# Attention with its weighing of v done for two key tiles in a row in odd steps

## The chip, the core and the metric

One core of a Trainium2 chip runs the whole layer: TensorE (PE) multiplies, ScalarE (ACT), VectorE (DVE) and GpSimd (POOL) work elementwise, SyncE's queue (SP) issues transfers. The metric is the device time of one execution in microseconds. The kernel before took 1863.95 us (median of three runs).

## The reference

A transformer layer with modulation, for 4 sequences of 1024 tokens and width 512, in fp32:

```
shift_msa, scale_msa, gate_msa, shift_mlp, scale_mlp, gate_mlp = split(silu(c) @ Wada.T + bada, 6)
h = modulate(rmsnorm(x, g1), scale_msa, shift_msa)
q, k, v = heads(h @ Wqkv.T + bqkv)              # 16 heads of 32
q = rmsnorm(q, gq) * 32 ** -0.5;  k = rmsnorm(k, gk)
o = softmax(q @ k.T) @ v
x = x + gate_msa * (o @ Wproj.T + bproj)
h = modulate(rmsnorm(x, g2), scale_mlp, shift_mlp)
x = x + gate_mlp * (gelu(h @ Wfc1.T + bfc1) @ Wfc2.T + bfc2)
```

## The kernel before

The kernel has three stages: a short setup, the attention (`build_attention`), and the second half with the output projection and the two large products (`build_mlp`). The change is in the attention alone.

The attention is one long row of 256 steps, L = 0 to 255, with 18 more (negative L) ahead of them for the first projections. A step is one key tile of 128 keys against 512 queries, for four heads at once. Eight steps (eight key tiles) make one half: four heads and 512 queries; 16 steps make one group of four heads, 64 steps one sequence. Each engine walks the same steps in its own order, which is written out by hand, and waits on semaphores for the others.

PE does in step L, in this order: `qk(L, 0)`, the scores of two heads (two matmuls); the first half of `fill`; `qk(L, 1)`, the scores of the other two heads; the row sums, in one step of eight; the second half of `fill`; in some steps a sum of squares or a turn; and at the end `weigh(L - 1)`, which multiplies the exponentials of the step before with v. A weighing is four 128x32 matmuls, one a head, into the four quarters of one PSUM bank; the profile shows each as two instructions. The row sums (`row_sums`) are 128x32 groups too, of ones with the summed exponentials. All else on PE has 128x128 weights.

`fill` does the projections that the coming groups and the next sequence need. `PLAN` lists them: units (q or k of four heads for 512 tokens) and tiles of v, each of 12 matmuls spread over two steps (six a step) or three (four a step). They all go through one PSUM bank, `gemm`. The first matmul of the next unit waits (`gemm_free`) until DVE has taken the last one out (`raw_out`, `v_out`). Every step from 1 to 207 has such projection work; steps 208 to 255 have none. A unit of q or k then goes on through square (ACT), sum of squares (PE), logarithm and root (ACT), the parts (DVE), and over DRAM into `k_stack` and `q_stack`. A turn (`turn`) transposes a normalised tile of x on PE.

ACT does the two exponentials of step L (`exponentials`), each for two heads, as soon as their scores are there. They go to a ring of three buffers `probs`, so that the exponential of step L waits for the weighing of step L - 3. PE's scores of a step wait for the exponential of the step before that reads the same PSUM tensor.

DVE adds up the exponentials (`add(L - 1)` in its step L, not for a half's first tile), and takes the projections out, in the order of its own list. The row sums of a half (`ROWS_AT`, the second step of the next half, always an odd one) need its last addition, and DVE's first addition of the next half needs the row sums.

Names in the profile: L456 scores, L469 weighing (`pv`), L486 row sums, L493 sum of squares, L500 turn, L521 and L534 projections, L616 exponentials, L681 additions, L712 and L722 the projection taken out, L767 and L769 parts.

Of the kernel before, what the change touches and what calls it, by code (L numbers as in the profile page):

```python
# [93 lines left out]
FILL = {step + i: (kind, b, g, x, i, steps) for step, steps, b, kind, g, x in PLAN for i in range(steps)}  # L94
# [8 lines left out]
def at_row(when):  # L103
    return {NT * (hh + 1) + when: hh for hh in range(NC * NG - 1)}


ROWS_AT, COMPACT_AT, INVERT_AT, INVERTED_AT, SPREAD_AT, OUT_AT = (at_row(x) for x in (ROWS, COMPACT, INVERT, INVERTED, SPREAD, OUT))
OUT_AT[AFTER + 1] = NC * NG - 1

TURN = list(range(-17, -9)) + [15, 19, 21, 23, 27, 35, 39, 45]  # L110
for b in range(2, B):
    TURN += [BSTEPS * b - 78 + 8 * t for t in range(NT)]
TURN_AT = {step: n for n, step in enumerate(TURN)}
STAT_AT, HOUT_AT, SPLIT_AT = ({step + after: n for step, n in TURN_AT.items()} for after in (-1, 1, 2))
MOD_AT = {TURN[NT * b - 1] + 2: b for b in range(1, B)}

# [156 lines left out]
def build_attention(nc, small, dram, wq_hi, wq_lo):  # L273
# [4 lines left out]
    with ExitStack() as ctx:  # L278
# [160 lines left out]
        def _(pe):  # L439
            issued = dict(units=0, v=0, squares=0, turns=0, rows=0)  # L440

            def qk(L, p):
                group, st = L // STEPS, L % STEPS
                half, j = st // NT, st % NT
                s = group % 2
                if p == 0:
                    if st == 0 or st == NT // 2:
                        pe.wait_ge(k_in[s][st // (NT // 2)], 64 * (group // 2 + 1))
                    if j == 0:
                        pe.wait_ge(q_in[half], 64 * (group + 1))  # L450
                if L > 0:

                    pe.wait_ge(exp_done, 2 * (L - 1) + p + 1)
                for i in range(2):
                    h = 2 * p + i
                    mm = nc.tensor.matmul(scores[p][:, i, :], k_stack[s][:, h, j * P:(j + 1) * P], q_stack[half][:, h, :],  # L456
                                          start=True, stop=True)
                mm.then_inc(qk_mm, 1)

            def weigh(l):  # L460
                b, g, j, hh = l // BSTEPS, l // STEPS % NG, l % NT, l // NT
                pe.wait_ge(exp_done, 2 * l + 2)
                if l % BSTEPS < NT:
                    pe.wait_ge(v_moved, b * NT + j + 1)
                if j == 0 and hh >= NH:

                    pe.wait_ge(o_done, hh - NH + 1)
                for h in range(HG):
                    mm = nc.tensor.matmul(pv[hh % NH][h * DH:(h + 1) * DH, :], v[b % 2][:, j, (g * HG + h) * DH:(g * HG + h + 1) * DH],  # L469
                                          probs[l % RING][:, h, :], start=(j == 0), stop=(j == NT - 1))  # L470
                mm.then_inc(pv_mm, 1)

            def aux_free():

                if issued["squares"]:
                    pe.wait_ge(ln_done, issued["squares"])
                if issued["turns"]:
                    pe.wait_ge(h_moved, issued["turns"])
                if issued["rows"]:
                    pe.wait_ge(rows_moved, issued["rows"])  # L480

            def row_sums(hh):
                pe.wait_ge(added, ADDS * (hh + 1))
                aux_free()
                for h in range(HG):
                    mm = nc.tensor.matmul(aux[h * DH:(h + 1) * DH, :], small["ones"][:], sums[:, h, :], start=True, stop=True)  # L486
                mm.then_inc(rs_mm, 1)
                issued["rows"] += 1

            def sum_squares(n):  # L490
                pe.wait_ge(sq_done, n + 1)
                aux_free()
                nc.tensor.matmul(aux[:], small["head_ones"][:], squares[:], start=True, stop=True).then_inc(ss_mm, 1)  # L493
                issued["squares"] += 1

            def turn(n):
                pe.wait_ge(x_normed, n + 1)
                aux_free()
                for k in range(KT):
                    mm = nc.tensor.transpose(aux[:, k * P:(k + 1) * P], xt[n % XS][:, k * P:(k + 1) * P], small["ident"][:])  # L500
                mm.then_inc(turned, 1)
                issued["turns"] += 1
# [36 lines left out]
            def fill(L, part):  # L539
                if L not in FILL:  # L540
                    return
                kind, b, g, x, i, steps = FILL[L]
                per = 3 * KT // steps
                lo = i * per + part * (per // 2)
                hi = lo + per // 2
                if kind == "v":
                    v_products(b, x, lo, hi)
                else:
                    unit_products(kind, b, g, x, lo, hi)

            for L in range(START, AFTER):
                if L >= 0:
                    qk(L, 0)
                fill(L, 0)
                if L >= 0:
                    qk(L, 1)
                if L in ROWS_AT:
                    row_sums(ROWS_AT[L])
                fill(L, 1)
                if L in SUM_AT:  # L560
                    sum_squares(SUM_AT[L])
                if L in TURN_AT:
                    turn(TURN_AT[L])
                if L > 0:
                    weigh(L - 1)
                if L == ADA_MM:
                    for k in range(KT):
                        for i, r in enumerate(ada_rows):
                            if k == 0:
                                pe.wait_ge(ada_w_in[i], 16)  # L570
                            mm = nc.tensor.matmul(scores[0][r, 0, :], silu[:, k, :], ada_w[i][:, k, :], start=(k == 0), stop=(k == KT - 1))
                    mm.then_inc(ada_mm, 1)
                if L == -1:

                    pe.wait_ge(ada_made, NA_LATER)
# [808 lines left out]
```

## Time and profile before

| | |
|---|---|
| median of three runs | 1863.95 us (1860.57 to 1865.57) |
| the profiled execution | 1864.95 us, span 1863.2 us |
| PE busy | 1760.5 us, 94% |
| DVE busy | 1101.3 us, 59% |
| ACT busy | 921.3 us, 49% |
| POOL busy | 363.3 us, 19% |
| attention, steps 1 to 255 | about 95 to 1005 us |
| of these, steps with projections | 95 to 877 us |

Times in the rows are microseconds from the span's start. PE's busy time is that of overlapping matmuls, with modelled ends: the distance between two starts tells what a matmul costs, not its duration. PEld is the loading of weights, which runs beside the matmuls. DVE and ACT are unevenly used: most of their work is in the attention. "Idle before" in brackets is the engine's idle time in front of a row and what ended it; "issue" is time in which the engine waited for nothing that the profile shows.

### The profile page before, as it was taken

What the parts mean: (1) busy time and instruction counts of PE and PEld (TensorE: products, weight loads), DVE (VectorE), ACT (ScalarE), POOL (GpSimd) and SP (SyncE); (2) the same over time, 40 slices, a digit from 0 to 9 for tenths busy, and PEclk for the clock granted to TensorE, in tenths of its full rate; (3) what the DMA queues carried; (4) which work ended last, traced back from release to release, by engine and by line L of the source; (5) the groups of instructions that cost most, each with busy time, mean ns of one, the idle gap of its engine ahead of it and who ended that gap; (6) DMA issues with size and microseconds to landing.
All of it is one profiled execution on the core that took longest, in us unless ns stands there. A gap on an engine that the chain in (4) does not pass through costs nothing. (4 is left out here: it accounts for less than half of the span.)

```text
span 1863.2 us, 23267 instructions
## 1 busy us (share of the span) xinstructions
PE 1760.5 (94%) x8368; PEld 1139.4 (61%) x8368; DVE 1101.3 (59%) x1343; ACT 921.3 (49%) x1110; POOL 363.3 (19%) x296
## 2 busy tenths in 40 slices
PE   3899899999999999999995799999999999999998
PEld 1555454555555555544231577888888787878786
DVE  4578878888898888878785654223232414232311
ACT  2277577777777777777885432222121222122221
POOL 1100100010110110000000432324241424233331
PEclk7999999999999999999997799999999999999999
DMA  5555535556555555454563331202020201001000
GB/s 184 153 146 142 138 107 139 137 138 157 132 132 144 135 144 128 126 133 137 132 134 103 116 102 40 63 6 62 17 62 17 62 17 51 28 30 44 6 29 23
DMA packets 137611, 176.69 MB, mean 95 GB/s; under 512 B 33668, under 2 KB 58244, under 8 KB 137528
## 3 DMA queue, kind: packets, MB, share of 16 engines
q1 hardware_dynamic: 122472, 158.79, 32.1%
q10 hardware_dynamic: 15056, 16.81, 2.8%
q8 instruction: 50, 0.82, 0.2%
q14 instruction: 33, 0.27, 0.1%
HBM read 124.63 MB, written 50.92 MB: 94 GB/s over the span
## 5 line engine op out<-in xcount | busy, mean ns | idle before, releaser
L616 ACT ACTIVATE probs<-scores,shift 128x1024 f32<-128x1024 f32 x512 | 549.7, 1115 | 195.6 <-PE scores L456 191.8
L681 DVE TENSOR_TENSOR sums<-sums,probs 128x2048 f32<-128x2048 f32 x192 | 444.5, 2315 | 45.0 <-ACT probs L616 40.7
L456 PE MATMUL scores<-q_stack,k_stack 128*128 128x512 f32 x1024 | 345.7, 423 | 6.6 <-ACT probs L616 6.5
L456 PEld LDWEIGHTS scores<-q_stack,k_stack 128*128 128x128 f32 x1024 | 169.6, 188 | 254.4 <-ACT probs L616 133.3
L1148 PE MATMUL acc<-w_hi,act_parts 128*128 128x512 f32 x1024 | 317.4, 391 | 0.0
L469 PE MATMUL pv<-probs,v 128*32 128x512 f32 x2048 | 274.3, 608 | 0.4 <-ACT probs L616 0.4
L1111 POOL TENSOR_TENSOR act_parts<-act_full,act_parts 128x512 fp32r<-128x512 f32 x128 | 169.6, 1325 | 501.7 <-ACT act_parts L1062 501.0
L1055 ACT ACTIVATE act_full<-up,f_bias 128x512 f32<-128x512 f32 x128 | 88.3, 690 | 337.7 <-PE up L1165 317.0
L1148 PEld LDWEIGHTS acc<-w_hi,act_parts 128*128 128x128 f32 x1024 | 190.7, 188 | 38.6
L1165 PE MATMUL up<-z_hi,w_hi 128*128 128x512 f32 x512 | 201.5, 394 | 5.1 <-POOL z_lo L1098 5.1
L1165 PE MATMUL up<-z_lo,w_hi 128*128 128x512 f32 x512 | 200.3, 391 | 0.0
L1165 PE MATMUL up<-z_hi,w_lo 128*128 128x512 f32 x512 | 200.2, 391 | 0.0
L1148 PE MATMUL acc<-w_lo,act_parts 128*128 128x512 f32 x512 | 199.4, 389 | 0.0
L1223 DVE TENSOR_TENSOR y_next<-proj,p_bias 128x512 f32<-128x512 f32 x28 | 19.3, 690 | 297.2 <-PE proj L1126 297.2
L1062 ACT ACTIVATE act_parts<-act_full 128x512 fp32r<-128x512 f32 x128 | 81.2, 635 | 222.1 <-PE acc L1148 221.0
L521 PE MATMUL gemm<-h_hi,wqkv_hi 128*128 128x512 f32 x256 | 103.9, 406 | 14.4 <-issue 11.6
L1165 PEld LDWEIGHTS up<-z_hi,w_hi 128*128 128x128 f32 x512 | 96.9, 189 | 25.5 <-POOL z_lo L1098 5.5
L469 PEld LDWEIGHTS pv<-probs,v 128*32 128x32 f32 x2048 | 41.1, 108 | 114.7 <-ACT probs L616 62.2
L658 POOL TENSOR_TENSOR x_inv<-x_sqc,minus_half 128x1 f32<-128x1 f32 x32 | 17.6, 551 | 475.9 <-DVE x_sqc L733 475.9
L1165 PEld LDWEIGHTS up<-z_lo,w_hi 128*128 128x128 f32 x512 | 97.0, 189 | 20.1
L1165 PEld LDWEIGHTS up<-z_hi,w_lo 128*128 128x128 f32 x512 | 96.8, 189 | 20.4
L1148 PEld LDWEIGHTS acc<-w_lo,act_parts 128*128 128x128 f32 x512 | 96.1, 188 | 20.2
(134 smaller groups left out, 2092.9 us busy)
## 6 DMA issues: line engine op xcount, KB each, us to landing
parts_scratch<-parts SPq DMA_DIRECT2D x64, 512.0 KB, 3.1
k_stack<-parts_scratch SPq DMA_DIRECT2D x128, 256.0 KB, 4.9
q_stack<-parts_scratch SPq DMA_DIRECT2D x128, 256.0 KB, 5.1
xt<-in_x SPq DMA_DIRECT2D x32, 256.0 KB, 2.9
heads_out<-o_out SPq DMA_DIRECT2D x32, 256.0 KB, 4.7
out<-result SPq DMA_DIRECT2D x32, 256.0 KB, 2.0
inverse<-inverse_scratch SPq DMA_DIRECT2D x124, 64.0 KB, 2.0
heads<-heads_out SPq DMA_DIRECT2D x30, 256.0 KB, 3.3
```

Of the source, the lines that this page charges most:

```text
L456: mm = nc.tensor.matmul(scores[p][:, i, :], k_stack[s][:, h, j * P:(j + 1) * P], q_stack[half][:, h, :], start=True, stop=True)
L469: mm = nc.tensor.matmul(pv[hh % NH][h * DH:(h + 1) * DH, :], v[b % 2][:, j, (g * HG + h) * DH:(g * HG + h + 1) * DH], probs[l % RING][:, h ...
L521: mm = nc.tensor.matmul(gemm[:], w[:, k, at:at + P], h[:, k, c], start=(n == 0), stop=(n == len(terms) - 1))
L616: nc.scalar.activation(probs[L % RING][:, 2 * p:2 * p + 2, :], scores[p][:], ACT.Exp, bias=small["shift"][:]).then_inc(exp_done, 1)
L658: nc.gpsimd.tensor_tensor(x_inv[:, t:t + 1], x_sqc[:, t:t + 1], small["minus_half"][:, 0:1], ALU.pow).then_inc(inv_done, 1)
L681: nc.vector.tensor_tensor(sums[:], a[:], probs[l % RING][:], ALU.add).then_inc(added, 1)
L1055: nc.scalar.activation(act_full[m % 2][:], up[m % 2][:], ACT.Gelu_apprx_tanh, bias=f1_bias[:, m:m + 1]).then_inc(gelu_done, 1)
L1062: nc.scalar.activation(act_parts[m % 2][:, 0, :], act_full[m % 2][:], ACT.Copy).then_inc(act_hi, 1)
L1111: nc.gpsimd.tensor_tensor(act_parts[m % 2][:, 1, :], act_full[m % 2][:], full(act_parts[m % 2][:, 0, :]), ALU.subtract).then_inc(act_lo, 1)
L1148: mm = nc.tensor.matmul(acc[t][:], act_parts[m % 2][:, b, t * P:(t + 1) * P], w2[a][:, m, :], start=(m == 0 and i == 0), stop=(m == NM - 1 ...
L1165: mm = nc.tensor.matmul(up[m % 2][:], w1[a][:, k, m * P:(m + 1) * P], z[b][:, k, :], start=(k == 0 and i == 0), stop=(k == KT - 1 and i == 2))
L1223: nc.vector.tensor_tensor(yt, proj[:], p_bias[:], ALU.add).then_inc(proj_moved, 1)
```

## The change

In steps up to 207 (`PAIRED`, the last one with projections) PE no longer weighs one tile at the end of each step. It weighs none in an even step and two in an odd one: `weigh(L - 2)` and `weigh(L - 1)`. The row sums of a half move from the middle of their step to directly in front of these weighings. From step 208 on the order is as before. No other engine's code is changed, and nothing is added or removed.

```
+PAIRED = max(FILL)
+assert PAIRED % 2 == 1
...
                 fill(L, 0)
                 if L >= 0:
                     qk(L, 1)
-                if L in ROWS_AT:
+                if L in ROWS_AT and L > PAIRED:
                     row_sums(ROWS_AT[L])
                 fill(L, 1)
                 if L in SUM_AT:
                     sum_squares(SUM_AT[L])
                 if L in TURN_AT:
                     turn(TURN_AT[L])
-                if L > 0:
+                if L in ROWS_AT and L <= PAIRED:
+                    row_sums(ROWS_AT[L])
+                if L > PAIRED:
+                    weigh(L - 1)
+                elif L > 0 and L % 2 == 1:
+
+                    if L > 1:
+                        weigh(L - 2)
                     weigh(L - 1)
```

## Rows read from the trace of the kernel before

**Rows 1.** Busy us by stretch: length, each engine (instructions), clock, DMA, GB/s

```profile
93.17:150.31 57.14, 56.33 (x278) 30.29 (x276) 43.60 (x40) 43.53 (x48) 0.00 (x0) 1.00 0.54 139
150.31:332.62 182.31, 169.31 (x836) 89.08 (x833) 153.21 (x187) 124.70 (x142) 16.82 (x18) 0.98 0.50 133
332.62:877.09 544.47, 543.00 (x2807) 278.98 (x2803) 464.13 (x464) 409.82 (x453) 45.23 (x30) 1.00 0.53 136
```

**Rows 2.** PE's timeline, steps with projections: start, us, what, idle before

```profile
501.65 0.39 PE L534 MATMUL gemm<-wqkv_hi,h_lo 128*128 128x512 f32 x1
501.97 1.07 PE L469 MATMUL pv<-probs,v 128*32 128x512 f32 x8
502.97 0.73 PE L456 MATMUL scores<-q_stack,k_stack 128*128 128x512 f32 x2
503.54 0.39 PE L534 MATMUL gemm<-wqkv_hi,h_hi 128*128 128x512 f32 x1
...
504.23 0.62 PE L456 MATMUL scores<-q_stack,k_stack 128*128 128x512 f32 x2
504.69 0.39 PE L534 MATMUL gemm<-wqkv_hi,h_hi 128*128 128x512 f32 x1
...
505.38 1.02 PE L493 MATMUL aux<-squares,head_ones 128*128 128x512 f32 x2
506.32 1.07 PE L469 MATMUL pv<-probs,v 128*32 128x512 f32 x8
```

**Rows 3.** Timeline of all engines in the tail, where row sums stand before a weighing

```profile
944.93 1.06 PE L486 MATMUL aux<-sums,ones 128*32 128x512 f32 x8
945.39 0.13 PEld L469 LDWEIGHTS pv<-probs,v 128*32 128x32 f32 x4 [0.30 <-ACT probs L616]
945.82 1.04 PE L469 MATMUL pv<-probs,v 128*32 128x512 f32 x8
...
946.79 0.96 PE L456 MATMUL scores<-q_stack,k_stack 128*128 128x512 f32 x3
```

**Rows 4.** PE's timeline, steps 88 to 91

```profile
450.16 0.72 PE L456 MATMUL scores<-q_stack,k_stack 128*128 128x512 f32 x2
...
454.80 1.07 PE L486 MATMUL aux<-sums,ones 128*32 128x512 f32 x8
455.79 0.50 PE L521 MATMUL gemm<-h_hi,wqkv_hi 128*128 128x512 f32 x1
456.13 0.39 PE L521 MATMUL gemm<-h_lo,wqkv_hi 128*128 128x512 f32 x1
...
459.18 0.39 PE L521 MATMUL gemm<-h_hi,wqkv_lo 128*128 128x512 f32 x1
...
461.50 0.40 PE L521 MATMUL gemm<-h_hi,wqkv_hi 128*128 128x512 f32 x1
```

**Rows 5.** DVE's timeline, steps 88 to 91

```profile
453.77 0.69 DVE L761 SCALAR_TENSOR_TENSOR raw<-norms,raw 128x512 f32<-128x512 f32 x1 [0.84 <-ACT norms L591]
...
457.24 0.55 DVE L738 TENSOR_SCALAR xt<-xt,x_inv,x_gain 128x512 f32<-128x512 f32 x1 [0.66 <-POOL x_inv L658]
...
459.90 0.74 DVE L712 TENSOR_SCALAR raw<-gemm,qk_bias 128x512 f32<-128x512 f32 x1
```

**Rows 6.** ACT's timeline, step 88

```profile
451.01 2.12 ACT L616 ACTIVATE probs<-scores,shift 128x1024 f32<-128x1024 f32 x2 [1.04 <-PE scores L456]
```

**Rows 7.** Timeline of all engines where a unit ends in step 140

```profile
638.55 0.75 DVE L712 TENSOR_SCALAR raw<-gemm,qk_bias 128x512 f32<-128x512 f32 x1 [0.78 <-PE gemm L521]
...
640.01 0.39 PE L521 MATMUL gemm<-h_hi,wqkv_hi 128*128 128x512 f32 x1
```

**Rows 8.** PE's timeline, step 23

```profile
190.37 0.48 PE L521 MATMUL gemm<-h_hi,wqkv_hi 128*128 128x512 f32 x1 [2.00 <-issue]
...
191.08 0.63 PE L521 MATMUL gemm<-h_hi,wqkv_lo 128*128 128x512 f32 x1
```

**Rows 9.** ACT's timeline, step 149

```profile
670.07 0.69 ACT L587 ACTIVATE norms<-aux,ln_floor 128x512 f32<-128x512 f32 x1 [2.41 <-DVE raw L761]
```

## The prediction

> **What bounds the kernel.** The page's first part says that PE is busy for nearly all of the span, but that is pipelined matmuls overlapping each other and doesn't say what one of them costs. So I began with the busy time by stretch [rows 1]. The change acts in the 207 steps with projections: steps 1 to 15 (57.1 us), 16 to 55 (182.3 us), 56 to 207 (544.5 us). In the last, PE is at its full clock and never idle for long, DVE is at 464.1 of 544.5 us (85%) and ACT at 75%. In the middle one PE is busy for 169.3 of 182.3 us, and DVE holds it up in nine steps. So PE's own work sets the time in most of the stretch, with DVE some 15% behind it.
>
> Next, PE's timeline inside steps [rows 2]. Two score matmuls and the next projection product are 0.46 us apart when nothing was switched (504.23 to 504.69), 0.23 us each. Around the weighing it is slower: the last product starts at 501.65, the weighing at 501.97, 0.09 us later than a pitch of 0.23; from there to the scores takes 1.00 us; the scores then take 0.57 us to the next product, 0.11 more than the undisturbed pair. The 128x32 groups of a weighing thus cost 1.20 us in a step.
>
> **What two in a row save.** Two such groups stand directly behind each other in the tail, where there is no projection between the row sums and the weighing: 944.93 to 945.82 is 0.89 us, and 945.82 to the scores at 946.79 is 0.97 us [rows 3]. Together 1.86 us, against 2 x 1.00 apart; and one entry (0.09) and one exit (0.11) go as well: 0.34 us a pair. The kinds of row differ (the first is the row sums, whose weights are all ones), but shapes and type are the same, so I take this price. At the low end of what it could be, only entry and exit go (0.20).
> Odd steps 3 to 207 are 103 pairs: 103 x 0.34 = 35.0 us. Step 1 weighs one tile alone.
>
> The Trainium skill (TensorE: Matmul & The Clock Gate, The mechanism) says that weight loads overlap running matmuls only where they go to other row groups; here every tile uses all 128 rows. The trace disagrees: the loads of the weighing start at 945.39, in the middle of the row sums [rows 3]. By the page the second group would start only when the first is over, at 1.06 us instead of 0.89, and the 103 pairs would bring 17.5 us in place of 35.0.
>
> **Row sums.** They now stand in the middle of a filled step: 0.99 us from 454.80 to the next product at 455.79, 0.34 from it to the one after, 0.11 over the pitch [rows 4], and with the entry of 0.09 that is 1.19 us. Directly in front of the weighing they cost 0.89 [rows 3]. 25 of them stand at or before step 207: 25 x 0.30 = 7.5 us. They come up to 1 us later in their step, but the new place is still in front of two weighings; ACT's copy of them and DVE's first addition of the next group wait for them, and both have until the next scores. Cost taken: nothing; without that cover a few tenths in each of 25 steps.
>
> No instruction is added or removed, no DMA is touched, and SP's and POOL's queues stay as they are. PE's gross gain is 42.5 us. Now what the weighing covered.
>
> **Exponentials.** An even step has no weighing. With four products it lasts 0.57 + 0.92 + 0.46 = 1.95 us. ACT's two exponentials of that step start 0.85 us after its first scores and end at 2.97 (451.01 + 2.12 against 450.16) [rows 4, 6]. The next step's second scores need the last: due at 1.95 + 0.92 = 2.87, free at 3.01. That is 0.14 us in each even step of four products with no turn or sum of squares at its end, 22 that end no projection unit: 3.1 us, of which two lie in the middle stretch. With six products the step is 2.41 us and nothing waits. The ring of three probability buffers costs nothing: the exponential of an even step needs the first weighing of the step before, which PE has done before it starts the scores.
>
> **The hand-over of the projection's bank.** This is the larger one. There is one bank for the projection, so the first product of a unit waits until DVE has taken the unit before. A unit that ends in an odd step gets more cover than now (two weighings), one that ends in an even step loses 1.2 us. Of 84 units 51 end in an even step. Kinds:
> - 12 with nothing behind their last product. DVE takes the bank at 638.55 for 0.75 us, and the next product at 640.01 comes 0.71 us after that [rows 7]. Of the 1.20 us of cover 0.5 was needed: 12 x 0.5 = 6.0 us.
> - 12 with a turn behind. For seven of them (steps 90, 98, 106, 114, 154, 162, 170) DVE's order decides. In the first, counted from 450.16: DVE's chain starts with the parts at 453.77, which wait for ACT's second exponential and root of that same even step, so PE's change doesn't bring it forward. It runs on, with one POOL wait of 0.66, to 459.90, and the bank is free at 460.64, +10.48 [rows 5]. PE will come earlier: step 88 takes 1.95, step 89 1.84 + 0.14 + 0.09 + 0.89 + 0.89 + 0.97 = 4.82, step 90 1.95 + 0.44 for the turn (461.50 less 459.18 is 2.32; less 0.23, 0.09, 0.99 and 0.57 it is 0.44 [rows 4]). With the scores it is at +9.62 and waits to +10.53: 0.9 us. 7 x 0.9 = 6.3 us, the others 0.4.
> - 27 with a sum of squares behind (505.38 to 506.32, less the entry: 0.85 us [rows 2]), which leaves 1.15 us to DVE's 0.8. Free where DVE comes at once; it doesn't in the middle stretch.
>
> **The middle stretch.** In nine of its steps PE now waits for DVE's copy, as at 190.37, 2.00 us [rows 8]. DVE's finish doesn't move when PE is quicker. And the weighing that stood ahead of that wait stands behind it now, so 0.9 us of cover becomes 0.9 us of work after it. What DVE still gains is that it sometimes waits for PE in turn. Of 20 x 0.34 + 5 x 0.30 = 8.3 us I keep 4.
>
> Two more pairs bring nothing: behind steps 84 and 148 ACT's logarithm waits for DVE (2.41 us before 670.07 [rows 9]), with the exponentials behind it in ACT's order and PE's next scores behind those: 0.7 us.
>
> **Sum.** Steps 1 to 15: 7 x 0.34 + 0.30 = 2.7, less 0.5 (step 2) and 0.6 (step 14): 1.6. Middle: 4. Steps 56 to 207: 76 x 0.34 + 19 x 0.30 = 31.5, less 20 x 0.14 = 2.8, 8 x 0.5 = 4.0, 6.3 + 0.4, 1.2 for two ends with a late DVE, 0.7: 16.1. Together 21.7 us. The profiled execution took 1864.95 us (span 1863.2), 1.0 above the median 1863.95; 1864.95 - 21.7 = 1843.25, and 1842 on the median's scale. I take 1843.
>
> **Rivals.**
> - *The whole 42.5 us* (chance 0.1): DVE's copies hide after all, since DVE's additions start earlier by the moved weighing. For it: DVE is idle for 15%. Against: the bank at 638.55 [rows 7], where DVE comes at once and still needs 0.75. About 1823 (1818 to 1829).
> - *DVE takes it all* (0.12): its waits for POOL and ACT (0.66 and 0.84 us [rows 5]) can't shrink. If it stays at 85 to 87%, steps 56 to 207 need 464.1 / 0.87 = 533 to 545 us, at most 11 us less than now; with 0 to 2 from the rest, 1852 to 1863. Against: nothing in PE's or DVE's order fixes that share.
> - *Second group as slow as the page's rule has it* (0.06; the trace speaks against it): a pair is 1.06 + 0.97 = 2.03 and with entry and exit saves 0.17, so 42.5 becomes 25.0; with the same losses, 20.8 us, the time would be about 1861.
> - *Slower* (0.05): the hand-over without cover. If each of the 51 even ends costs the whole 1.20 us, that is 61 us against 42.5: 1883. It decides from 0.84 us an end; the kinds above need 0.5 for the commonest and 0.9 for seven. In the middle stretch it could come true, since PE's idle time there grows from 2.0 to nearly 3 us, and after such a wait a product takes 0.63 us instead of 0.40, and the granted clock of the stretch is 0.98 [rows 1, 8].
> - *The forecast* (0.67): its own range 1834 to 1851, from the middle stretch at 0 to 8 us, the hand-over at half or all again.
>
> **Numbers.** Change by over 0.3% is 5.6 us, about what a measurement of this kernel can tell. Range 1829 to 1857. Faster 0.87, same 0.08, slower 0.05.
>
> **What would show it.** After: from a pair's first weighing to the second about 0.89 us, from there to the scores 0.97 to 1.00; even steps of four products near 1.95 to 2.0 us; a wait of 0.5 us before the first product after units ending in even steps, released by DVE; 0.9 us at the seven turn steps; DVE at 87 to 89% in steps 56 to 207; the tail and the second stage as long as now. I am wrong if the weighing pair is 2.0 us or more, if PE's waits for DVE or ACT in steps 56 to 207 sum to over 25 us or under 8, or if more of the middle stretch runs at the lower clock.

## The result, and the profile after

The changed kernel takes 1848.78 us (median of six executions, 1847.01 to 1852.23), the kernel before 1863.29 (six, 1860.57 to 1865.57). The ratio is 0.9927, 95% interval [0.9916, 0.9938]: 13.6 us less by the ratio, between 11.6 and 15.7 (the two medians are 14.5 apart). The profiled execution took 1848.84 us with a span of 1847.0. Forecast were 1843 us and a range of 1829 to 1857.

The page's first part, engine by engine (busy us, share of the span, instructions):

```profile
PE 1729.6 (94%) x8368; PEld 1154.5 (63%) x8368; DVE 1101.5 (60%) x1343; ACT 913.2 (49%) x1110; POOL 358.7 (19%) x296
```

PE is busy for 31 us less than before, while the span is only 16 us shorter. PE's busy time fell by twice as much as came out at the end; the rest went into waits. The windows of the same stretches as [rows 1] say where:

```profile
147.64:327.08 179.44, 162.53 (x843) 92.69 (x841) 153.89 (x188) 124.90 (x145) 19.42 (x18) 0.99 0.52 136
327.08:860.58 533.50, 522.66 (x2806) 288.79 (x2802) 466.28 (x465) 403.91 (x451) 37.91 (x30) 1.00 0.54 139
```

In [rows 1] PE was busy for 543.0 of 544.5 us in steps 56 to 207, now for 522.7 of 533.5: 20.3 us of work gone, and 10.8 us of idle time in place of 1.5. DVE has as much to do as before and stands at 87% (466.28 / 533.50).

The sharpest table is made from PE's timeline, one execution of each kernel: the distance in us between the first scores of step 1, 16, 56, 208 and 255.

| steps | before | after | gain | forecast |
|---|---|---|---|---|
| 1 to 15 | 59.72 | 58.48 | 1.2 | 1.6 |
| 16 to 55 | 177.85 | 173.53 | 4.3 | 4 |
| 56 to 207 | 544.47 | 533.51 | 11.0 | 16.1 |
| 208 to 254 | 120.43 | 120.57 | -0.1 | 0 |

Next, the pair itself. This is PE's timeline over an odd step of four products (start, length, then the instruction):

```profile
788.27 0.73 PE L458 MATMUL scores<-q_stack,k_stack 128*128 128x512 f32 x2
788.84 0.40 PE L523 MATMUL gemm<-h_lo,wqkv_hi 128*128 128x512 f32 x1
...
789.30 0.70 PE L458 MATMUL scores<-q_stack,k_stack 128*128 128x512 f32 x2
789.84 0.39 PE L523 MATMUL gemm<-h_hi,wqkv_hi 128*128 128x512 f32 x1
...
790.39 1.92 PE L471 MATMUL pv<-probs,v 128*32 128x512 f32 x16
792.24 0.50 PE L458 MATMUL scores<-q_stack,k_stack 128*128 128x512 f32 x1
```

The two weighings stand as one row (x16). In the view from 791.46 on the second stands by itself:

```profile
791.27 1.04 PE L471 MATMUL pv<-probs,v 128*32 128x512 f32 x8
```

From the first weighing to the second 790.39 to 791.27, 0.88 us; from there to the scores 0.97. Forecast were 0.89 and 0.97 from the tail [rows 3]. By the Trainium skill's rule on weight loads (TensorE: Matmul & The Clock Gate, The mechanism), which lets them overlap running matmuls only towards other row groups, the second would have come 1.04 us after the first; by that rule this trace disagrees, as the one before did. The same section of the Trainium skill also lets a load into the background weight buffer be pulled ahead, which would allow what the trace shows. The scores of this step also stand further from their products than the 0.46 us of [rows 2]: 0.57 and 0.54, since each of them was held a little by the exponentials (the second one ends at 789.22, and the weights of the second scores are loaded from 789.27).

Now what the missing cover costs. The timeline of all engines where a unit ends in step 132, which [rows 7] show for step 140 of before:

```profile
624.32 0.74 PE L458 MATMUL scores<-q_stack,k_stack 128*128 128x512 f32 x2
624.66 0.19 PEld L523 LDWEIGHTS gemm<-h_hi,wqkv_lo 128*128 128x128 f32 x1
624.90 0.40 PE L523 MATMUL gemm<-h_hi,wqkv_lo 128*128 128x512 f32 x1
...
626.35 0.30 PEld L458 LDWEIGHTS scores<-q_stack,k_stack 128*128 128x128 f32 x2 [0.33 <-ACT probs L625]
626.35 0.73 PE L458 MATMUL scores<-q_stack,k_stack 128*128 128x512 f32 x2
626.49 0.75 DVE L721 TENSOR_SCALAR raw<-gemm,qk_bias 128x512 f32<-128x512 f32 x1 [0.72 <-PE gemm L523]
...
627.31 0.19 PEld L523 LDWEIGHTS gemm<-h_hi,wqkv_hi 128*128 128x128 f32 x1 [0.67 <-issue]
...
627.34 0.47 PE L523 MATMUL gemm<-h_hi,wqkv_hi 128*128 128x512 f32 x1 [0.26 <-issue]
...
627.65 0.40 PE L523 MATMUL gemm<-h_lo,wqkv_hi 128*128 128x512 f32 x1
```

Three things are to be seen. The next step's scores (626.35) wait for ACT: 2.03 us after the step's first, not 1.95. Then PE stands until DVE has taken the bank: the copy begins at 626.49, is over at 627.24, and the product comes at 627.34, 0.99 us after the scores. In [rows 7] it came 0.71 us after the copy's end, with a weighing in between. The profile puts this wait down to "issue"; that it is the copy is shown below, where the copy is made shorter. And the two products after the wait are 0.31 us apart instead of 0.23: the weights of the first were loaded only at 627.31, 0.03 us ahead of it, where in the stream they are there 0.24 ahead (624.66 for 624.90).

### The profile page after: what moved, and what is told of

It reads as the page before. It is cut to its first block and busy times, and to the rows that moved or that the text cites. A ratio compares the mean times of both kernels' runs of the same rounds, so it can differ in the third digit from the quotient of the medians.

```text
span 1847.0 us, 23267 instructions
## 1 busy us (share of the span) xinstructions
PE 1729.6 (94%) x8368; PEld 1154.5 (63%) x8368; DVE 1101.5 (60%) x1343; ACT 913.2 (49%) x1110; POOL 358.7 (19%) x296
## 5 line engine op out<-in xcount | busy, mean ns | idle before, releaser
L690 DVE TENSOR_TENSOR sums<-sums,probs 128x2048 f32<-128x2048 f32 x192 | 449.1, 2339 | 31.3 <-ACT probs L625 26.5
L458 PE MATMUL scores<-q_stack,k_stack 128*128 128x512 f32 x1024 | 357.4, 434 | 7.4 <-ACT probs L625 7.1
L471 PE MATMUL pv<-probs,v 128*32 128x512 f32 x2048 | 251.6, 600 | 0.4 <-ACT probs L625 0.4
L471 PEld LDWEIGHTS pv<-probs,v 128*32 128x32 f32 x2048 | 54.2, 109 | 131.9 <-issue 100.2
```

The costliest lines, as they stand in the source:

```text
L690: nc.vector.tensor_tensor(sums[:], a[:], probs[l % RING][:], ALU.add).then_inc(added, 1)
```

## The experiments

Each kernel was timed beside the kernel before, whose medians were between 1863.56 and 1864.35. The last four columns are the distances of the table above, from each kernel's own profiled execution. The edits are shown against the changed kernel, if nothing else is said.

| kernel | median us | ratio [95%] | 1-15 | 16-55 | 56-207 | 208-254 |
|---|---|---|---|---|---|---|
| row sums moved only | 1855.20 | 0.9956 [0.9942, 0.9969] | 59.39 | 175.94 | 538.49 | 118.79 |
| pairs only | 1852.72 | 0.9943 [0.9930, 0.9957] | 58.80 | 175.65 | 537.17 | 120.24 |
| one tile alone at even ends | 1838.56 | 0.9862 [0.9847, 0.9877] | 58.14 | 173.14 | 526.02 | 120.06 |
| uneven products | 1848.12 | 0.9916 [0.9902, 0.9929] | 58.50 | 173.05 | 532.25 | 118.81 |
| pairs where they cover | 1842.91 | 0.9889 [0.9872, 0.9905] | 59.17 | 170.14 | 529.87 | 120.40 |
| before, half additions | 1840.72 | 0.9872 [0.9856, 0.9889] | 59.17 | 162.43 | 542.79 | 116.22 |
| change, half additions | 1818.74 | 0.9757 [0.9741, 0.9774] | 57.32 | 159.79 | 524.61 | 116.24 |
| pairs in the tail too | 1863.13 | 0.9991 [0.9982, 1.0001] | 58.55 | 175.64 | 533.56 | 134.83 |
| both rules | 1841.68 | 0.9875 [0.9857, 0.9893] | 58.14 | 172.87 | 530.23 | 121.14 |
| quarter copy | 1837.01 | 0.9853 [0.9835, 0.9870] | 57.33 | 171.84 | 526.54 | 120.60 |
| both rules, two at most | 1837.21 | 0.9856 [0.9839, 0.9872] | 58.10 | 171.17 | 526.20 | 121.13 |

Two things limit what the stretches say. The last one has the same code in all kernels but one, and yet stands between 118.8 and 121.1 us (116.2 with half additions). And in steps 16 to 55 the granted clock differs from execution to execution: 0.98 for the kernel before, pairs only, one tile alone, pairs in the tail too and both rules; 0.99 for the change, row sums only, uneven products and quarter copy; 1.00 for the other four. In steps 56 to 207 it is 1.00 in all of them.

Some terms: a pair of steps is an even step and the odd one behind it, and its gain is by how much the two together became shorter. A pure end is an even step that ends a projection unit and has nothing behind its last product; a turn end is one with a turn behind it. The seven turn ends are those that the prediction names.

**The two halves of the change.** The row sums alone:

```
-                if L > PAIRED:
-                    weigh(L - 1)
-                elif L > 0 and L % 2 == 1:
-                    if L > 1:
-                        weigh(L - 2)
+                if L > 0:
                     weigh(L - 1)
```

> Only the row sums move to directly in front of the weighing; one tile is weighed in every step. My theory (PE pays for each change between 128x32 and 128x128 groups): 25 row sums save 0.30 us each, 7.5 us less than before, about 1856, with the sums at 0.88 to 0.89 us from their first matmul to the weighing's. Rival (the gain of the change comes from the order of the row sums alone): 14 us less, 1849. Rival (the later row sums hold up ACT's copy and DVE's next addition): 0 to 3 us less.

And the pairs alone, the row sums left in the middle of their step:

```
-                if L in ROWS_AT and L > PAIRED:
+                if L in ROWS_AT:
                     row_sums(ROWS_AT[L])
-                if L in ROWS_AT and L <= PAIRED:
-                    row_sums(ROWS_AT[L])
```

> Only the pairs of weighings in odd steps; the row sums stay in the middle of their step. My theory: 103 x 0.34 = 35 us saved on PE, about 26 us given back at the hand-over of the projection's bank, at the exponentials and in steps 16 to 55, so 7 to 9 us less than before, about 1855, that is the whole change less the 7.5 us of the row sums. Rival (row sums alone): as before within 2 us, 1863.

PE's timeline with the row sums moved, step 89:

```profile
451.89 1.07 PE L488 MATMUL aux<-sums,ones 128*32 128x512 f32 x8
452.78 1.04 PE L471 MATMUL pv<-probs,v 128*32 128x512 f32 x8
453.75 0.74 PE L458 MATMUL scores<-q_stack,k_stack 128*128 128x512 f32 x2
```

0.89 us from the row sums to the weighing. Each such step is 0.34 to 0.35 us shorter in steps 56 to 207 (two of the 19 by 0.37), not 0.30. Together these steps bring 6.0 us, since the pair at 62 loses 0.56 in return. The pairs alone bring 7.3 us there. The sum of the two, 13.3, is more than the change's 11.0, and the trace says where the difference lies: at the seven turn ends a pair of steps loses 0.27 us with the row sums in their old place and 0.61 with them moved. DVE's chain there hangs on an earlier start, so what the row sums save in the pair before is waited away at the end: 7 x 0.34 = 2.4 us, about the whole difference. (Two more, 0.36 us at step 66 one way and the 0.56 at 62 the other, nearly cancel.)

**Cover given back.** In even steps that end a unit, with no sum of squares behind, one tile is weighed at the end as before:

```
+SINGLE = {step + steps - 1 for step, steps, *_ in PLAN}
+SINGLE = {L for L in SINGLE if L > 0 and L % 2 == 0 and L not in SUM_AT}
...
-                if L > PAIRED:
-                    weigh(L - 1)
-                elif L > 0 and L % 2 == 1:
-                    if L > 1:
-                        weigh(L - 2)
-                    weigh(L - 1)
+                if L > 0:
+                    held.append(L - 1)
+                if L > PAIRED or L % 2 == 1 or L in SINGLE:
+                    for l in held:
+                        weigh(l)
+                    held.clear()
```

> As the whole change, but in an even step that ends a projection unit with no sum of squares behind it (24 of them) the tile held is weighed there, and the odd step after it weighs only its own. My theory (a pair across such an end loses 0.3 us where nothing stands behind the last product and 0.6 where a turn does, against a step-by-step order): steps 56 to 207 win back 3.7 + 4.5 = 8 us, the whole takes 1840 to 1842. Rival (DVE's throughput sets the time in these steps): the waits only move, 1847 to 1850. Rival (the exponentials are the larger loss): at most 3 us less than the whole change.

All engines at step 132 of this kernel:

```profile
621.67 0.39 PE L526 MATMUL gemm<-h_hi,wqkv_lo 128*128 128x512 f32 x1
...
621.99 1.06 PE L474 MATMUL pv<-probs,v 128*32 128x512 f32 x8
622.10 0.75 DVE L724 TENSOR_SCALAR raw<-gemm,qk_bias 128x512 f32<-128x512 f32 x1 [0.70 <-PE gemm L526]
...
622.98 0.73 PE L461 MATMUL scores<-q_stack,k_stack 128*128 128x512 f32 x2
...
623.55 0.39 PE L526 MATMUL gemm<-h_hi,wqkv_hi 128*128 128x512 f32 x1
```

DVE's copy (622.10 to 622.85) runs beneath the weighing, the product at 623.55 waits for nobody. Steps 56 to 207 fall by 18.4 us against before, 7.5 more than in the change; the pairs of steps at pure ends and turn ends stand within 0.02 us of before, where most of them were 0.3 to 0.6 behind, but for step 124 (-0.52). This kernel beats both, by 25.7 us against before and by 10 (medians) or 12 (ratios) against the change, a little more than was expected.

**Is it the copy's length, or the switch itself?** DVE takes out a quarter of the columns; the other three quarters of q and k are left stale.

```
+                c = CH if n < 2 else P
-                nc.vector.tensor_scalar(raw[n % 2][:], gemm[:], ...)
+                nc.vector.tensor_scalar(raw[n % 2][:, 0:c], gemm[:, 0:c], ...)
```

> The whole change, with DVE taking out only 128 of the 512 columns of a q or k unit (from the third unit on; the rest of the buffer keeps what an earlier unit left), so the copy takes about 0.3 us instead of 0.75. My theory (in the pairs 76, 132, 140, 178, 196 and 204, where DVE comes at once, the copy's own length is what PE waits for): each such pair gets back 0.3 to 0.45 us, to about level with before, and a wait for the exponentials of 0.26 stays; in all 1838 to 1842. Rival (PE waits there for something else: the exponentials, or the change of groups): these pairs stay 0.3 us longer than before, 1847 to 1850.

```profile
619.18 0.73 PE L458 MATMUL scores<-q_stack,k_stack 128*128 128x512 f32 x2
619.32 0.35 DVE L722 TENSOR_SCALAR raw<-gemm,qk_bias 128x128 f32<-128x128 f32 x1 [0.72 <-PE gemm L523]
...
619.77 0.47 PE L523 MATMUL gemm<-h_hi,wqkv_hi 128*128 128x512 f32 x1
...
620.08 0.40 PE L523 MATMUL gemm<-h_lo,wqkv_hi 128*128 128x512 f32 x1
```

The copy takes 0.35 us in place of 0.75, and the product comes 0.59 us after the scores, not 0.99. The pure ends but step 124 (-1.00) come out at +0.05 to +0.08 us against before instead of -0.29 to -0.36: what an even step of four products gives that ends nothing (0.07 to 0.08). So what a pure end loses beyond that is the copy's own length. The seven turn ends come out at -0.20 instead of -0.61, which is the 0.40 us by which the copy at the end of DVE's chain is shorter. The time, 1837.01, is 1 us below what was expected.

**Does DVE's whole load bind?** Here both kernels add only half of the exponentials (the row sums are of half):

```
-                nc.vector.tensor_tensor(sums[:], a[:], probs[l % RING][:], ALU.add).then_inc(added, 1)
+                nc.vector.tensor_tensor(sums[:, 0:2, :], a[:, 0:2, :], probs[l % RING][:, 0:2, :], ALU.add).then_inc(added, 1)
```

> The kernel before, with DVE adding up the exponentials of two of the four heads only (the other two are left out of the sums), so each addition takes about half of its 2.3 us. My theory: steps 56 to 207 stay as they are (PE bound, 544.5 us, less about 2), steps 16 to 55 lose most of their waits for DVE, 12 to 17 us, and the tail its 5 us at step 217; about 1842. Rival (DVE's throughput bounds everything): 40 us or more.

> The whole change, with the same halved additions. My theory: with DVE early the turn pairs no longer lose 0.6 us and the middle stretch keeps its 8 us, but the pairs across a unit's end with nothing behind it still lose 0.3 us each, because there DVE comes at once and its copy itself takes 0.75 us; the difference to the kernel before with halved additions grows from 15 to 23 to 27 us, about 1818. Rival (the losses are ACT's and PE's own): the difference stays at 14 to 16 us.

```profile
154.44:316.87 162.43, 160.99 (x814) 85.55 (x810) 109.77 (x178) 121.38 (x139) 17.45 (x17) 1.00 0.55 143
316.87:859.66 542.79, 542.79 (x2807) 279.31 (x2803) 320.83 (x464) 409.13 (x453) 28.76 (x30) 1.00 0.54 136
```

```profile
152.63:312.42 159.79, 154.12 (x814) 89.56 (x810) 108.66 (x177) 119.99 (x139) 18.39 (x17) 1.00 0.55 144
312.42:837.03 524.61, 522.48 (x2807) 289.08 (x2803) 320.97 (x464) 403.35 (x451) 29.56 (x30) 1.00 0.55 141
```

Steps 56 to 207 of the kernel before (the first two rows are its windows, the others those of the change) hardly move: DVE goes from 464 to 321 us of work and the stretch from 544.5 to 542.8. With pairs it falls from 533.5 to 524.6: the change is worth 18.2 us there instead of 11.0. What came back are the ends where DVE came late (turn ends +0.11 us a pair of steps, step 124 -0.37); the pure ends still lose 0.31 to 0.34, since there DVE comes at once and only its copy counts. In steps 16 to 55 DVE's load does set the time: 15 us less without the change, of which some is the granted clock (0.98 in the one execution, 1.00 in the other). But with a quick DVE the change brings only 2.6 us there where about 8 were expected. Of the 20 pairs of steps 12 gained 0.28 to 0.63 us, so there the pair pays as elsewhere, and two 0.08 to 0.10; the ends at 28, 30 and 38 stand at -0.06 to -0.45, as pure ends do, and the pairs at 20, 22 and 52 at 0 to -0.86, with DVE light.

**Fewer products in the even step.** Where a unit takes three steps, the step without a weighing gets five or six products, the other two or three:

```
+                if L > 0 and steps == 3:
+                    counts = [(2, 3), (2, 0), (2, 3)] if (L - i) % 2 == 0 else [(2, 1), (3, 3), (2, 1)]
...
```

(The numbers in brackets are the products ahead of a step's second scores and behind them.)

> As the whole change, but units of three steps give their 12 products out as 5, 2, 5 (even, odd, even) or 3, 6, 3 (odd, even, odd) in place of 4, 4, 4, so that an even step has five or six. My theory (in an even step of four products PE comes to the next scores before the exponentials are done: a pair of steps 60 and 61 gained 0.08 us where 0.34 was saved, so 0.26 goes there): about 20 such pairs win back 0.26 us each, 5 us less than the whole change, 1843 to 1845. Rival (the loss is in the pair of weighings itself): no change, 1848 to 1850.

```profile
619.79 1.04 DVE L768 TENSOR_SCALAR h_full<-aux,scale,mod 128x128 f32<-128x128 f32 x3
...
621.09 1.10 PE L495 MATMUL aux<-squares,head_ones 128*128 128x512 f32 x2 [0.27 <-DVE h_full L768]
```

All 20 pairs of steps with four products and nothing behind the even one got back what they had lost to the exponentials. In 14 of them the pair has one product fewer and gained 0.42 to 0.48 us against the change, of which a product is 0.23; in the other six it has one more and still gained 0.03 to 0.07. That is 20 x 0.25 = 5 us, as meant, but steps 56 to 207 are only 1.3 quicker. The rest went again where a turn stands: nine turn ends lost 0.20 to 0.26 us with as many products as before, and the pairs at 74, 130 and 138, which have a turn in the even step, lost 0.22 to 0.24 with one fewer. PE comes too early there: the row at 621.09, in step 131, waits 0.27 us for DVE's work behind the turn. The time shows nothing, 1848.12 against 1848.78, where 1843 to 1845 was expected.

**Where else pairs pay.** In the last 48 steps, with no projections (`PAIRED = AFTER - 1`):

> As the whole change, with pairs up to step 255. Steps 208 to 255 have no projections; a step is 2.12 or 2.56 us there and ACT's two exponentials need 2.0 to 2.1. My theory: ACT runs dry during two weighings in a row (1.85 us) and then holds up the even step, so the tail grows by 0.3 to 0.8 us a pair, 7 to 20 us in all, 1856 to 1869. Rival (the switch saved counts here as well): 24 x 0.34 = 8 us less, 1841.

ACT's timeline there, after one row of ACT in the tail of the kernel before:

```profile
952.33 4.25 ACT L616 ACTIVATE probs<-scores,shift 128x1024 f32<-128x1024 f32 x4 [0.44 <-PE scores L456]
```

```profile
921.82 4.14 ACT L625 ACTIVATE probs<-scores,shift 128x1024 f32<-128x1024 f32 x4 [1.39 <-PE scores L458]
927.35 4.14 ACT L625 ACTIVATE probs<-scores,shift 128x1024 f32<-128x1024 f32 x4 [1.39 <-PE scores L458]
932.88 1.11 ACT L625 ACTIVATE probs<-scores,shift 128x1024 f32<-128x1024 f32 x1 [1.39 <-PE scores L458]
```

PE's timeline there, where the next scores wait for the exponentials:

```profile
928.52 0.73 PE L458 MATMUL scores<-q_stack,k_stack 128*128 128x512 f32 x2 [0.82 <-ACT probs L625]
```

Without projections ACT has about as much to do as PE: before, four exponentials took 4.25 of 4.68 us for two steps, and ACT waited 0.44. With pairs it waits 1.39 us for scores that stand behind two weighings, and then PE waits for ACT: 5.53 us for two steps. The tail gets 14.4 us longer, and the whole gain is gone.

**Pairs wherever they cover.** Two are held until they are wanted, at either parity, and a unit's end or the row sums always bring them out. Against the kernel with cover given back:

```
-                if L > PAIRED or L % 2 == 1 or L in SINGLE:
+                if L > PAIRED or len(held) == 2 or L in SINGLE or L in ROWS_AT:
```

(`SINGLE` without its `L % 2 == 0`.)

> Tiles are held in either kind of step and weighed when two are held, at the end of a projection unit with no sum of squares behind it, and in the steps of the row sums; so in steps 1 to 8 the pairs stand in the even steps, which end the units, and every unit's end without a sum of squares has a weighing behind it. My theory (a weighing behind a unit's last product is cover for DVE's copy, and is wasted elsewhere): nothing lost against e3_single_at_ends in steps 56 to 207 and a few us won or lost elsewhere, 1835 to 1840. Rival (only odd steps suit, because row sums and the ring of three fit them): slower than e3_single_at_ends by 5 us or more.

1842.91, behind the kernel with cover given back and outside what was expected. Steps 16 to 55 are 3.0 us quicker than there, but at a granted clock of 1.00 against 0.98, so the order is not shown to be the reason. Steps 56 to 207 are 3.9 us slower, with as many pairs of weighings by the code (57). The reason is which step is left without one. Steps 91 to 93 take 2.01, 4.84 and 3.03 us, where with cover given back they take 3.04, 2.41 and 4.17: there the bare step is 92, which has a sum of squares behind it, here it is 91, with four products and nothing behind, and the exponentials' wait is paid, 0.26 us. Eleven such places lose 0.26 to 0.29 us each, 3.0 of the 3.9.

So the rule was used in steps 16 to 55 alone:

```
+SINGLE = {L for L in SINGLE if L > 0 and (L % 2 == 0 or 16 <= L < 56) and L not in SUM_AT}
...
+                if L > PAIRED or L in SINGLE or (len(held) == 2 or L in ROWS_AT if 16 <= L < 56 else L % 2 == 1):
```

> The order of e3_single_at_ends in steps 1 to 15 and 56 to 207, that of e7_pairs_where_they_cover in steps 16 to 55, where it ended 3.0 us earlier (step 56 at 170.1 instead of 173.1 us after step 16). My theory (each stretch on its own is set by its hand-overs): 3 us less than e3_single_at_ends, 1835 to 1837. Rival (what is won in the middle stretch is lost behind it by a later DVE): 1838 to 1840.

```profile
333.67 1.07 PE L491 MATMUL aux<-sums,ones 128*32 128x512 f32 x8
...
334.55 2.33 PE L474 MATMUL pv<-probs,v 128*32 128x512 f32 x20
...
335.66 1.11 ACT L628 ACTIVATE probs<-scores,shift 128x1024 f32<-128x1024 f32 x1 [5.09 <-PE pv L474]
```

This missed the 1835 to 1837 expected, by a fault of its own: at the seam three tiles were held to step 57, and the exponential (335.66) waited 5.09 us, until the first of them had been weighed and a buffer of the ring was free. The row of PE ahead of it is the run of three weighings, cut off by the view's end (20 of its 24 instructions). In steps 16 to 55, with the granted clock at 0.98 like that of the kernel with cover given back, the rule is worth 0.3 us (172.87 against 173.14). With `L < 55` in the same line the seam holds two:

> e9_both_rules with its seam mended: it had three tiles (54, 55, 56) held until step 57, and the exponential of step 57 waited 5 us for their weighing, because there are three buffers of them. Here no more than two are ever held. My theory (that wait is what e9 lost behind step 56): steps 56 to 207 take 526 to 527 us as in e3_single_at_ends, steps 16 to 55 170 to 173 us depending on the waits for DVE, in all 1836 to 1839, level with e3_single_at_ends or up to 3 us better. Rival (the order of the middle stretch itself makes DVE late behind it): steps 56 to 207 stay over 528 us.

Steps 56 to 207 are back at 526.20 and 16 to 55 at 171.17, 2 us below the kernel with cover given back, again at a granted clock of 1.00 against 0.98; the whole, 1837.21 against 1838.56, is not told apart from it by the intervals.

## Why the forecast held, step by step

**Two in a row: 0.34 us a pair.** Shown. Where nothing else moves (20 pairs in steps 56 to 207: six products, or a sum of squares behind), the gain was 0.33 to 0.36 us.

**Row sums: 0.30.** 0.34 to 0.35 in 17 of 19 places, as the kernel with these alone shows: the same price as the pair. The place in front of two weighings cost nothing that the trace shows, but by the turn ends.

By kind of even step, in steps 56 to 207, the gain of the two steps from it on, beside what the forecast's terms make of it:

| even step | pairs | forecast | measured |
|---|---|---|---|
| ends a unit, nothing behind | 8 | -1.3 | -3.7 |
| ends a unit, turn behind | 11 | -3.0 | -4.5 |
| ends a unit, sum of squares behind | 7 | +1.5 | +2.6 |
| four products, nothing behind | 20 | +8.8 | +7.0 |
| six products | 13 | +5.0 | +4.6 |
| turn or sum of squares behind, no end | 17 | +5.1 | +4.9 |
| sum | 76 | +16.1 | +11.0 |

**Exponentials: 0.14 us.** Mis-sized. The pair gained 0.07 to 0.08, so 0.26 went: the next step's scores come 0.08 late, the second scores later again, and the restart behind each wait costs on its own (scores to product 0.57 and 0.54 instead of 0.46). I counted the one wait that I had seen. That it is the exponentials' wait is shown by the uneven products, which won it back.

**Hand-over: 0.5 us at a pure end.** The mechanism was right, the size wrong: seven of the eight cost 0.63 to 0.70. The working took the cover needed (the copy) and left out that the even step itself runs 0.08 later and that two products behind the wait are 0.08 further apart. That is 1.2 us of the 2.4 in the table's first line. The other 1.2 us are step 124 alone (-1.39), which was counted as a common pure end. DVE was still in an addition when PE's last product was there, and this addition was itself slow. The kernel before and the change at the same step:

```profile
579.15 2.29 DVE L681 TENSOR_TENSOR sums<-sums,probs 128x2048 f32<-128x2048 f32 x1 [0.33 <-ACT probs L616]
579.72 2.88 POOL L653 TENSOR_TENSOR h_lo<-h_full,h_hi 128x512 fp32r<-128x512 f32 x1 [8.14 <-ACT h_hi L607]
581.36 0.74 DVE L712 TENSOR_SCALAR raw<-gemm,qk_bias 128x512 f32<-128x512 f32 x1
```

```profile
567.16 1.47 POOL L662 TENSOR_TENSOR h_lo<-h_full,h_hi 128x512 fp32r<-128x512 f32 x1 [6.22 <-ACT h_hi L616]
567.57 3.20 DVE L690 TENSOR_TENSOR sums<-sums,probs 128x2048 f32<-128x2048 f32 x1
...
569.23 0.40 PE L523 MATMUL gemm<-h_hi,wqkv_lo 128*128 128x512 f32 x1
...
570.70 0.74 DVE L721 TENSOR_SCALAR raw<-gemm,qk_bias 128x512 f32<-128x512 f32 x1
...
571.54 0.47 PE L536 MATMUL gemm<-wqkv_hi,h_hi 128*128 128x512 f32 x1 [1.28 <-issue]
```

Before, the addition began first and took 2.29 us, and POOL's subtraction beside it 2.88. In the change the subtraction begins first and takes 1.47, and the addition 3.20. So of the 1.2 us some 0.9 are the longer addition (an estimate, 3.20 less 2.29), behind which the copy stands; the change turned round which of the two comes first. With half additions this pair loses 0.37 and not 1.39.

**Turn ends: 0.9 us at seven, 0.4 for the others.** The seven lost 0.60 to 0.64 us each against -0.56 forecast: right, and for the reason given, since half the additions or the single weighing removes the loss. The four others were guessed at 0.4 in all and cost 1.5 (step 66 alone -0.49).

**Sum of squares behind the end.** 1.1 us better than forecast: I had held 1.2 us against two late copies that didn't show.

**Steps 84 and 148.** 0.7 us, forecast to bring nothing: they bring 0.01 to 0.02. But ACT's lateness stays in the next pair as well (86 and 150: 0.05 and 0.02 instead of 0.34), 0.6 us more that I hadn't followed.

**Steps 1 to 15: 1.6 us.** 1.2 measured. Step 2 cost 0.68 us for 0.5; step 14 cost 0.33 for 0.6, a figure for which the prediction gave no row.

**The middle stretch: 4 us.** 4.3 measured, but the agreement is partly luck: with half additions, where the granted clock is 1.00 in both executions, the change brings 2.6. The pair at step 28 alone gained 2.4, and there the two executions differ in more than the order of work. The windows of step 29 (length, then busy time by engine, and the granted clock ninth; before, then after):

```profile
217.53:224.76 7.23, 5.30 (x22) 2.21 (x18) 6.74 (x6) 2.30 (x3) 1.31 (x1) 0.77 0.28 101
```

```profile
214.77:220.73 5.96, 4.51 (x27) 2.03 (x25) 5.43 (x7) 3.27 (x4) 1.34 (x1) 1.00 0.26 93
```

A granted clock of 0.77 is a stretch in which part ran at the lower of the two levels: there the second scores and their products take 1.91 us to the weighing instead of 1.25, and one weighing takes 1.86 us to the scores (222.90 to 224.76), as long as two in the change. That is 1.5 us. Another 0.6 is DVE's: one of its operations ahead of the copy took 1.66 us (217.88) instead of 0.75, with POOL at work beside it. Such stretches of the lower level fall at different steps in different kernels' executions (none in four of the thirteen, one or two in the others), so steps 16 to 55 say little below 2 us. That PE's wait now stands in front of two weighings is to be seen in step 53 (the pair at 52 lost 0.85 us):

```profile
311.82 1.03 PE L458 MATMUL scores<-q_stack,k_stack 128*128 128x512 f32 x2
315.47 0.47 PE L523 MATMUL gemm<-h_hi,wqkv_hi 128*128 128x512 f32 x1 [2.63 <-issue]
```

**The rivals.** The whole 42.5 us: out, by the waits above. DVE takes it all: its time, 1852 to 1863, is not far off, DVE's share did rise to 87%, and steps 56 to 207 took 533.5 us, which its 533 to 545 just holds. But that share is no limit, since with cover given back it is 88% (463.74 us of 526.02); steps 56 to 207 don't follow DVE's load (464 to 321 us of work moved before by 1.7), and the pure ends lose as much with half the additions. DVE matters by when it comes at an end, not by how much it has to do. The second group at the page's price: out, 0.88 us. Slower: out as a whole; a pure end costs 0.63 to 0.70, or 0.94 to 0.98 at the seven turn ends, and it would take 0.84 over all 51.

In all, the mechanisms named were those that acted in steps 56 to 207, but for the addition and the subtraction beside it at step 124, which the prediction didn't have. The 5 us between forecast and result are sizes: the exponentials (20 x 0.12) and the hand-over (7 x 0.16) taken too small, step 124 (1.2) and step 66 taken for common ones, ACT's lateness followed one pair too short (0.6), against row sums and sums of squares that did better. The 4 us of the middle stretch are right in part by the clock. PE's idle time of 10.8 us in steps 56 to 207 is within the 8 to 25 that I had set, and the granted clock of the middle stretch is no lower than before (0.99, 0.98); the losses were larger than the idle time, because the spacing behind each wait grew too. What stays open is why the pairs at 20, 22 and 52 bring nothing even with half the additions.

## What to carry to other kernels

When small groups in another shape are put together, ask of each place they leave what they covered: here the cheap rule (two at a time, but one where a bank is handed over) brought 25.7 us, the plain one 13.6. Which step is left bare counts too: 3 us lay between leaving one with a sum of squares behind and one with nothing. And a wait costs more than its length: count the late start behind it too, some 0.1 us at the first matmul pair and again at the next. Where another engine has as much to do, as ACT in the last 48 steps, the same grouping is a pure loss. All of this is from one kernel.

## What the runs showed of the hardware

A weighing by itself among 128x128 products costs 1.20 us of PE's time, in a row with another 0.88 and 0.97 with the way out. The Trainium skill says that a change of tiling mode drains the engine (TensorEngine Tiling (Array Packing), Key Properties). The trace agrees as to direction, with 0.34 us for each run of such groups that was merged into another, the row sums too.

I had not expected the restart: behind a wait that the bank or an exponential ends, the next weights are loaded only then (the load at 627.31, its matmul at 627.34), and two matmuls that stand 0.23 us apart in a stream stand 0.31 apart (627.34, 627.65). Behind an exponential it is about the same: the scores of 788.27 are 0.57 us from their product instead of 0.46.

Nor had I seen that POOL reaches DVE's additions. In the change 11 of the 224 additions take 2.63 to 3.42 us, the others 2.22 to 2.29, and these 11 are those that begin while POOL's subtraction for `h_lo` is running. Where the addition begins first it keeps its 2.29 us, and the subtraction grows instead, from 1.3 us alone to as much as 3.26. In the trace before it is the same, with 10. No kernel was run without the subtraction, so this rests on the order in the traces.
